# Second attention of a two-layer transformer kernel: the first row scores of an iteration placed behind its first projection

## What is computed

```python
q = (x @ Wq.T).reshape(B, S, 32, 16).transpose(0, 2, 1, 3)
k, v = _split_kv(x @ Wk.T, B, S), _split_kv(x @ Wv.T, B, S)
q = q * cos + rotate_half(q) * sin
k = k * cos + rotate_half(k) * sin
scores = jnp.einsum('bhqd,bhkd->bhqk', q, k) / jnp.sqrt(jnp.float32(16))
allowed = (j <= i) & (j > i - 128)
attn = softmax(where(allowed, scores, -inf))
out = einsum('bhqk,bhkd->bhqd', attn, v) @ Wo.T
```

## Time and profile before

| | |
|---|---|
| median of 3 runs | 741.8 us (741.8 to 742.43) |
| profiled execution, its own time | 742.59 us |
| its span, first to last instruction | 740.7 us |
| mean granted TensorE clock | 0.907 |
| busy: PE, DVE, ACT, POOL | 84%, 52%, 37%, 32% |
| second attention, from its first row scores to its last output matmuls | about 242 to 529 us |

### The profile page before, as it was taken

One profiled execution on the slowest core, in us unless ns is written; L12 is line 12 of the kernel. 1 busy time (PEld: TensorE's weight loads), 2 busy tenths in 40 slices (PEclk: granted clock), 3 DMA queues, 4 the chain that ended last, 5 costly groups with the idle time before them and its releaser, 6 DMA issues.

```text
span 740.7 us, 13453 instructions
## 1 busy us (share of the span) xinstructions
PE 618.5 (84%) x5108; PEld 487.0 (66%) x5108; DVE 388.8 (52%) x1120; ACT 277.7 (37%) x439; POOL 236.5 (32%) x347
## 2 busy tenths in 40 slices
PE   2998996648889886989898987778689899999984
PEld 2997985536677664766676665556448688878761
DVE  4324345285776766758585766561546043322354
ACT  5156046356644143334342533344620022221313
POOL 6003422354200235445352634354005511111062
PEclk9999999688999986989898999576889999999997
DMA  8921213323016727263452719120005859997455
GB/s 292 401 94 34 50 31 100 79 56 94 1 60 153 141 74 145 79 95 114 61 144 31 171 40 213 22 67 23 1 1 177 334 198 395 418 417 291 184 169 185
DMA packets 49360, 104.37 MB, mean 141 GB/s; under 512 B 12113, under 2 KB 18385, under 8 KB 47761
## 3 DMA queue, kind: packets, MB, share of 16 engines
q1 hardware_dynamic: 30032, 61.68, 23.4%
q0 software_dynamic: 13744, 31.61, 18.8%
q10 hardware_dynamic: 5520, 10.23, 3.8%
HBM read 63.77 MB, written 35.13 MB: 134 GB/s over the span
## 4 chain that ended last, share of the span: by engine, by line
PE 56%; DVE 11%; DMA 11%; ACT 9%; issue 7%; POOL 6%; SPq 1%; POOLq 0%; ACTq 0%; DVEq 0%
PE bank L331 14%; PE bank L508 10%; PE bank L367 10%; ACT FP L1427 3%; DVE FP L902 3%; PE bank L594 3%; PE bank L579 3%; DMA slots_out<-FP 3%; PE bank L566 3%; PE bank L378 2%; POOL slots_in L1825 2%; POOL FP L1837 2%; DMA QS<-QS 2%; PE bank L389 2%; PE bank L709 2%
## 5 line engine op out<-in xcount | busy, mean ns | idle before, releaser
L1427 ACT ACTIVATE FP<-bank 128x512 f32<-128x512 f32 (+1 forms) x250 | 145.8, 624 | 324.2 <-PE bank L579 132.5
L1160 DVE CUSTOM_DVE_ANT_0 kraw<-bank,maskb 128x256 bf16<-128x256 f32 (+1 forms) x256 | 88.5, 401 | 60.6 <-PE bank L566 60.6
L508 PE MATMUL bank<-W,XR 128*128 128x512 f32 x348 | 106.0, 450 | 0.1
L331 PE MATMUL bank<-FP 128*128 128x128 f32 x558 | 87.5, 311 | 1.3 <-ACT FP L1427 1.3
L367 PE MATMUL bank<-W,XR 128*128 128x512 f32 x288 | 78.9, 420 | 6.1 <-DVE W L902 5.2
L508 PEld LDWEIGHTS bank<-W,XR 128*128 128x128 f32 x348 | 71.1, 216 | 16.3 <-DVE XR L902 0.5
L1789 POOL TENSOR_SCALAR_AFFINE_SELECT FP<-FP 128x512 f32<-128x512 f32 x64 | 41.4, 669 | 114.3 <-ACT FP L1427 114.3
L367 PEld LDWEIGHTS bank<-W,XR 128*128 128x128 f32 x288 | 63.7, 271 | 11.8 <-DVE W L902 5.6
L331 PEld LDWEIGHTS bank<-FP 128*128 128x128 f32 x558 | 65.2, 192 | 3.5 <-issue 1.8
L902 DVE TENSOR_TENSOR FP<-FP,bank 128x128 f32<-128x128 f32 (+1 forms) x39 | 14.4, 369 | 70.5 <-ACT FP L1427 45.7
L331 PE MATMUL bank<-RP,W 128*128 128x512 f32 x192 | 47.5, 404 | 4.4 <-DVE FP L902 2.2
(11 more groups left out here) (164 smaller groups left out, 1021.9 us busy)
## 6 DMA issues: line engine op xcount, KB each, us to landing
FP<-in_experts_dram SPq DMA_DIRECT2D x31, 768.0 KB, 7.1
slots_out<-QS SPq DMA_DIRECT2D x48, 256.0 KB, 2.7
FP<-slots_in POOLq DMA_DIRECT2D x31, 256.0 KB, 6.5
slots_out<-FP ACTq DMA_DIRECT2D x31, 256.0 KB, 7.7
slots_in<-RP SPq DMA_DIRECT2D x7, 1024.0 KB, 13.3
RP<-slots_out POOLq DMA_DIRECT2D x16, 384.0 KB, 5.7
QS<-slots_out POOLq DMA_DIRECT2D x10, 384.0 KB, 8.4
FP<-in_shared_dram SPq DMA_DIRECT2D x4, 768.0 KB, 7.5
```

Of the source, the lines that this page charges most:

```text
L331: mm = nc.tensor.matmul(bank, lhs, rhs, start=(n == 0), stop=(n == len(terms) - 1))
L508: mm = nc.tensor.matmul(b[:, :], *terms[n], start=(n == 0), stop=(n == len(terms) - 1))
L1160: ins = nc.vector.tensor_tensor_reduce(masked[:, 2 * (f % 2) + m, 0:n], b[:, m, :], maskb[:, m0:m0 + n], 1.0, -BIG, ALU.add, ALU.max, hmax ...
L1427: return nc.scalar.activation(o, i, func, **kw)
```

## The change

It moves calls in the streams of PE, DVE and POOL and removes or adds none. In iterations 0 to 5 the row scores of step 0 stand behind the first key scores, the context rows and the key projection of that step, directly ahead of the row scores of step 1. On DVE the maxima of step 0 stand behind the division of the context. In iteration 6 (`late = 1`) every row score stands one step later, the last behind step 7's weighing; the maxima's split, transpose, copy and stack of the first half move a step too. Iteration -1 is unchanged.

```diff
@@ PE @@
-                t, r, d = i + 2, i + 1, i - 1
+                t, r, d, late = i + 2, i + 1, i - 1, int(i == T - 2)
                 for s in range(8):
-                    if r < T:
-                        row_scores(r, s)
+                    if r < T and (s > 0 or i < 0) and s >= late:
+                        row_scores(r, s - late)
                     if i >= 0 and (s % 2 == 0 or i >= 1):
                         key_scores(i, 2 * (s // 2), s % 2)
                     if s < 2 and d >= 0:
                         context_rows(U, d, s)
                     if s < 2 and 2 <= t < T:
                         project2(t, 1 - s)
+                    if s == 0 and 0 <= i < T - 2:
+                        row_scores(r, 0)
...
-                    if s == 5 and r < T:
+                    if s == 5 + late and r < T:
                         turn_maxima(r, 0)
...
+                if i == T - 2:
+                    row_scores(r, 7)
@@ DVE @@
-                    if r < T:
-                        row_maxima(r, s)
+                    if r < T and (s > 0 or i < 0) and s >= late:
+                        row_maxima(r, s - late)
                     if s < 2 and d >= 0:
                         context_divided(U, d, s)
+                    if s == 0 and 0 <= i < T - 2:
+                        row_maxima(r, 0)
...
-                    if s == 3 and r < T:
+                    if s == 3 + late and r < T:
                         maxima_split(r, 0)
...
-                    if s == 5 and r < T:
+                    if s == 5 + late and r < T:
                         maxima_out(r, 0)
...
-                    if s == 7 and r < T:
+                    if s == 7 and r < T and late == 0:
                         maxima_split(r, 1)
...
                 if i == T - 2:
+                    row_maxima(r, 7)
+                    maxima_split(r, 1)
                     shared_low(0)
                     shared_low(1)
@@ POOL @@
-                    if step == 6 and r < T:
+                    if step == 6 + late and r < T:
                         stack_maxima(r, 0)
```

More of the change, by code:

```diff
@@ L1802, in _ @@
             for i in range(-1, T):
-                t, r = i + 2, i + 1
+                t, r, late = i + 2, i + 1, int(i == T - 2)
                 for step in range(8):
```

## The result

The changed kernel takes 764.04 us (four runs, 760.96 to 768.56) against 741.88 us before (741.8 to 742.43): a ratio of 1.0302, with an interval of 1.025 to 1.0354. It is 22.2 us slower. The profiled execution is the longest of the four, 768.56 us, with a span of 766.1 us and a mean granted clock of 0.896 (before 740.7 us and 0.907), so its parts add up to 25.4 us and not to 22.2.

What follows compares the result with a forecast made beforehand. The prediction took the key scores' wait for the maxima transfer as the last to end in each iteration; -1.1 + 12.9 + 5.6 + 1.5 = 18.9 us on the median of 741.8 gave 760.7 us, range 750 to 767.

Steps and rivals of the forecast that it cites:

- The wait that ends last stays in front: Start of iterations: the maxima land after the stack, so the key scores, now first, still wait for the later transfer.
- Front, -1.1 us: Start of iterations: key scores begin 0.25 us earlier in iterations 0, 1, 3, 5 and 0.1 us in iteration 6.
- The new neighbour, +12.9 us: Iterations 0 to 5: second row scores wait for VectorE to read the banks, 2.15 us after the first, six times.
- The clock, +5.6 us: Second projection behind the new pause: clock falls in four of six iterations, costing 1.4 us each.
- the upper bound: Clock term's highest case: falls behind all six pauses at 1.9 us each, 11.4 us.
- A fall behind every pause: Second projections: by the skill's rule all six pauses would pay a clock fall, making the sum 2.8 us higher.
- Iteration 6 and its end, +1.5 us: End of iteration 6: last maxima come 3.0 us later, VectorE's adding and statistics fill 1.5 us, 1.5 us remain.
- a sign of being wrong: Iteration 6: the forecast is wrong if its end moves against its start by more than 3 us.
- The sum: Whole kernel: the four terms together make it 18.9 us slower, forecast as 760.7 us.
- its own signs: New profile: key scores wait for maxima, second row scores wait about 1.8 us, iteration distance grows 2 to 4 us.
- The faster rival, 4%: Start of iterations: maxima land early, key scores start 3.8 us earlier; 4.6 us faster, 737.2 us; chance 4%.

Runs made afterwards that it cites:

- e11: The changed kernel itself, unaltered, run and profiled again beside the later experiments: 766.7 us, against 743.15 us for the kernel before.
- e5: Against e1: six of the second projection's twelve matmuls moved into the pause between the first two calls of row scores; 757.83 us.
- e1: The change in iterations 0 to 5 only, iteration 6 left as in the kernel before: 761.64 us, against 743.36 us before.
- e8: The changed kernel with GpSimd issuing the first half's maxima ahead of the query stack: 740.52 us, ratio 0.9986 to the kernel before.
- e4: Against e1: six matmuls whose result is thrown away put into the pause between the first two calls of row scores; 756.46 us.
- e2: The change in iteration 6 only, iterations 0 to 5 left as in the kernel before: 742.31 us, against 743.36 us before.
- e6: The kernel before with GpSimd issuing the first half's maxima ahead of the query stack: 738.67 us, against 744.3 us before.
- e9: Against e1: maxima issued ahead of the query stack, first row scores placed after 8 of the first projection's 12 matmuls; 729.71 us.

## Why the prediction was right, and where it was not

**The forecast (760.7, 750 to 767 us) holds the result, 764.04, 3.3 us above its centre.** By its own steps:

- *The wait that ends last stays in front.* Right in the mechanism. The maxima landed last before iteration 3 again, by 0.8 us, and the first key scores of iterations 1 to 5 waited 1.65 to 4.59 us for them.
- *Front, -1.1 us.* Too small to be confirmed. That stretch shows -2.9 us and the waits at the starts -0.5 us, but by the clock and not by an earlier start. Iterations 3 and 4 gain 5.3 us, most of it in the first projection (2.98 and 3.01 us at a clock that had stayed high, against 4.86 and 4.93), and iterations 2 and 5 give back 2.5 us, mainly where that of iteration 5 takes 5.26 us against 3.70. In e11 none of the six first projections is faster than 4.3 us. The prediction had no clock in this term.
- *The new neighbour, +12.9 us.* Right to the hundredth, 2.15 us six times, since the same two calls stand at the same distance in the earlier trace rows. That no later wait takes it up is right too, and e5 shows why: it is VectorE's queue that is late.
- *The clock, +5.6 us.* The right size on average, with a scatter that the prediction did not have. The number of slow second projections was four of six in the prediction; four profiles have the same six pauses, with three (the result), four (e1), five (e8) and five (e11). Above 3.0 us each, these projections add 3.6, 4.0, 7.3 and 5.5 us. The +6.1 us of the stretches behind the pause hold only 3.6 us of that; the rest lies further on in the iterations. The size per fall was 0.7 to 2.2 us, so the 1.9 us that the upper bound counts for a projection was exceeded once, by one of 5.15 us in e8; its total of 11.4 us was not. That the falls of the second projection come from the pause did hold, since none is left when it is filled (e4).
- *A fall behind every pause.* The Trainium skill, page TensorE: Matmul & The Clock Gate, section "A second HAM failure mode: psum-queue depth-cycling", says that such short pauses make the clock swing between its two levels. The traces agree with the swinging (1.00 and 0.67 in the two windows above, both behind the same pause). That every such pause would be followed by a fall was the prediction's reading of it, and this did not hold: 7 of the 24 second projections ran at 3.0 us behind a pause of 1.65 us.
- *Iteration 6 and its end, +1.5 us.* Mis-sized: the traces have 0.17 us (e2) and 0.21 us (e11). The delay of the last maxima was 2.6 us and not 3.0, the adding and statistics filled 1.5 us of it as reckoned, and the conversion that closes the maxima took 0.9 us less, which the prediction did not have. The stretch still cost 4.8 us in the first profiled execution, over the 3 us that the prediction set as a sign of being wrong. This was the clock (0.50 against 0.62 before), not the order, since the same kernel does not show it in e11.
- *The sum.* By its own signs the forecast is met only on average. The distance from one iteration's first key scores to the next should have grown by 2 to 4 us. In the result's trace it grows by 4.22, 2.18, 4.29, 0.08, -0.52 and 5.35 us in iterations 0 to 5, and between iterations 3 and 4, the pair that the prediction named, it stays (33.83 before, 33.91 after). In e11 that pair has 38.87 us. So two executions of one kernel reach almost the same time, one with 15.6 us of its difference in iterations 0 to 5 and 9 us behind them, the other with 25.0 us in them. That four terms with such a scatter add up to within 3.3 us of the median is in part luck; the term of 12.9 us is not.
- *The faster rival, 4%.* Its mechanism was real and its condition false in the changed kernel. e8 makes the condition true. It lands 3.8 us below its kernel before by the medians and 1 us by the ratio, where the rival's arithmetic gave 4.6; its interval holds no change as well, so the nearness proves nothing. What I misjudged is why the maxima are late. "The maxima are issued behind the same stack" names the wrong neighbour: they are issued behind masks that wait for ScalarE.

**What stays open:** why the clock falls behind some pauses of 1.65 us and not behind others (of the four profiles, none has a fall behind that of iteration 1), what set it in iteration 6 of the first profile, and where all of e6's gain lies. The 4.9 us in and behind iteration 7 are not the change's: e11 has 247.4 us there, the kernel before 247.8.

## What to carry to other kernels

Before moving work out of the way of a wait, find which of two waits ends last and why its transfer starts when it does; here, once the key scores stood first, two lines in GpSimd's order, and not the order on TensorE, held the start of each iteration. Two calls that use the same banks need the consumer's whole reading time between them, and filling the producer's pause with work gains only what the clock costs, as long as the consumer's queue is the chain. One profile is not a budget: two executions of the changed kernel at the same time had their losses in different places, so take a second before sharing a difference out. A place in the middle of a long operation (8 of 12 matmuls) can be better than either end: late enough for one input, early enough for the consumer.

## What was not expected of the hardware

A pause of the same 1.65 us was followed by a second projection of 3.0 us in some iterations and of 3.7 to 4.6 us in others of the same execution (3.85 to 5.15 us in e8). And six matmuls in each of six pauses, whose results nobody reads, made a kernel 5.2 us faster (e4 against e1, 756.46 against 761.64 us): the mean granted clock rose from 0.892 to 0.901 in the runs of e1 to 0.911 to 0.914 in those of e4. A conversion of 128x16 numbers on VectorE took 1.06 us at one place in its order and 0.17 us at another (before and e2). The maxima transfer took 5.0 us to land even ahead of the stack, not the 1.9 us of the earlier trace rows, and 9.5 to 11.2 us ahead of iteration 6 in the profiles of before, the change, e6, e8 and e9, so its place saved time by its start and not by its length.
